# Value products of a fused attention kernel: issued after the second maximum and score of their half step, not between the two

## The chip, the cores and the metric

The kernel runs on one core of one Trainium2 chip. The metric is the device time of one launch in microseconds (us). Engines are named as in the profile: PE is TensorE (PEld its weight loads), DVE is VectorE, ACT is ScalarE, POOL is GpSimd, SP is SyncE.

## The reference

Sixteen sequences of 512 tokens, width 512, pass four residual layers, each on a layer norm of its input: a gated delta rule with 16 heads, a feed-forward layer with routed low-rank adapters, an attention layer, and the feed-forward layer again.

```
x = x + delta_rule(layernorm(x))
x = x + ffn(layernorm(x))
x = x + attn_b(layernorm(x))
x = x + ffn(layernorm(x))

# attn_b, the layer that the change is in (4 groups of queries x 8 key heads, 16 wide)
scores = einsum('bsqhd,bthd->bqhst', qh, kh) * scale
probs  = softmax(scores, axis=-1)
a_dot  = einsum('bqhst,bthd->bsqhd', probs, vh)
a_mem  = sigma_q @ memory / (sigma_q @ memory_norm)
out    = a_dot * (1 - w) + a_mem * w
```

## The kernel before

The program has two parts. The first is the delta rule layer over all 16 sequences; it leaves its result in memory. The second, `token_layers`, does the other three layers, one sequence (a batch) after the other, in a hardware loop of eight passes with two batches each. The change is in the attention of the second part and so runs 16 times.

Attention has 32 query heads. For each head the softmax needs a maximum for every query, and the kernel computes the score matrix twice: once with queries on the partitions, to take the maxima (`maximum`, L1333: one 128x512 matmul for each of four blocks of 128 queries, read by a DVE reduction, L1611), and once with keys on the partitions and the negated maximum already inside the operand (`score`, L1346: one 128x512 matmul for each of four blocks of keys, read by an ACT exponential, L1165, which writes `probs`). `values` (L1358) multiplies the exponentials of four heads with the values, four matmuls side by side, each 32 rows of the output; it does this in four blocks for a quad of heads, one for each block of keys, and adds them up in PSUM bank 6.

All engines run lists written in order. PE's is one Python loop over g = 0 to 44, with two half steps j = 0, 1 for each g. In half step j PE does two maxima of head g and two scores of head g - 7. In this text a **pair** is one maximum with the score issued behind it; a half step has two pairs and a g has four. The pattern repeats every four g, which makes sixteen pairs; they are numbered here 0 to 15 from a g that leaves 3 when divided by 4. In that cycle also stand:

- four value blocks, **V0 to V3**, in the half steps that `AV_SLOTS` names: the second half step of the first three g (pairs 2 and 3, 6 and 7, 10 and 11) and the first one of the fourth (pairs 12 and 13);
- **TURN** (L1405), four transposes of the finished quad, at the end of the first g, behind pair 3, and behind them the DVE's `av_rc` (L1601) and `av_n` (L1605) and POOL's addition (L1067);
- **MAXT** (L1385), four small transposes of the maxima, between the maximum and the score of pair 6. ACT copies them negated into `shift` (L1172), and SP moves that by DMA into the row of `q_stack` that the scores use three g later.

Waits that matter: scores use PSUM banks 0 to 2 in turn, so score m waits for the exponential of score m - 3 (L1345). Maxima use banks 3 to 5, so maximum m waits for the reduction of maximum m - 3 (L1332). MAXT and TURN share bank 7, so MAXT waits for `av_n`. `probs` has room for seven heads (`PROBS = 7`), so the first exponential of heads 7, 11, ..., 31 waits until V3 of a quad has read what it will overwrite:

```
if h >= PROBS and tt == 0:
    act.wait_ge(av_mm, at(b, QUADS, (h - PROBS) // 4 + 1))
```

Those heads are scored in the very g whose first half step holds V3: the exponential that waits is that of pair 12. Behind the exponentials of pairs 12 and 13, and ahead of that of pair 14, ACT's list has the copy of the finished values, `av_sb` (L1178), which V0 and TURN wait for. There are seven such heads in each batch. Five of them come while maxima still run (g = 14, 18, 22, 26, 30), and two later (g = 34, 38), since maxima end with g = 31 and scores with g = 38.

Of the kernel before, what the change touches and what calls it, by code (L numbers as in the profile page):

```python
# [847 lines left out]
QUADS = NQ * NKV // 4  # L848
# [6 lines left out]
AV_LAG = SCORE_LAG + 1  # L855
AV_SLOTS = ((0, 1), (1, 1), (2, 1), (3, 0))
# [9 lines left out]
def token_layers(nc, dims, x2_in, w_ffn, b_ffn, lora_b, gate_b, w_q, w_kv, mem_aug_in, mem_w_in, ident_in, rank_mask_in, sel_in, head_rows_in, out):  # L866
# [3 lines left out]
    with ExitStack() as ctx:  # L870
# [100 lines left out]
        def at(b, per, k):  # L971

            return b * per + k
# [7 lines left out]
        def turned_before(quad):  # L981

            return sum(4 * q + 3 + TURN_LAG < 4 * quad + MAXT_LAG for q in range(QUADS))

        def maxima_before(quad):

            return sum(4 * q + MAXT_LAG <= 4 * quad + 3 + TURN_LAG for q in range(QUADS))
# [197 lines left out]
        def _(pe):  # L1185
# [23 lines left out]
            with pe.Fori(0, NBATCH // 2) as bb:  # L1209
                for par in range(2):  # L1210
# [84 lines left out]
                    def pick_q(m):  # L1295
                        n, hp = divmod(m, HP)
                        if hp == 0:
                            pe.wait_ge(qlo_ready, at(b, NQ, n + 1))
                        bank = stack_bank(HP + m)
                        pe.matmul(ps[:, bank, :], sel[:, hp, :], q_hi[:, n, :], start=True, stop=False)  # L1300
                        pe.matmul(ps[:, bank, :], sel[:, HP + hp, :], q_lo[:, n, :], start=False, stop=True).then_inc(qsel_mm, 1)  # L1301
# [3 lines left out]
                    def memory(t):  # L1305

                        if t == 0:
                            pe.wait_ge(qelu_ready, at(b, NQ, NQ))
                            pe.wait_ge(qlo_ready, at(b, NQ, NQ))
                            pe.wait_ge(shift_ready, at(b, QUADS, 1))  # L1310
                        else:
                            pe.wait_ge(amem_ready, at(b, NT, t))
                        for n in range(NQ):
                            c0 = (DKV + 1) * (n % 2)
                            last = pe.matmul(ps[:, 6 + n // 2, c0:c0 + DKV + 1], q_elu[:, n, P * t:P * t + P],  # L1315
                                             mem_aug[:, :], start=True, stop=True)
                        last.then_inc(mem_mm, 1)

                    def pair(h):

                        n, kv = divmod(h, NKV)
                        return n * HP + kv // 2, kv

                    def maximum(g, st):

                        qt, kv = pair(g)
                        m = NT * g + st
                        if m in (1, 2):
                            pe.wait_ge(qrelu_ready, at(b, NQ, m))
                            pe.wait_ge(qlo_ready, at(b, NQ, m))  # L1330
                        elif m >= MAX_BANKS:
                            pe.wait_ge(max_ready, at(b, NT * NH, m - MAX_BANKS + 1))  # L1332
                        pe.matmul(ps[:, STACK_BANKS + m % MAX_BANKS, :], q_stack[:, qt, P * st:P * st + P], k_stack[:, kv, :],  # L1333
                                  start=True, stop=True).then_inc(max_mm, 1)

                    def score(h, tt):

                        qt, kv = pair(h)
                        if h == 0 and tt == 0:
                            pe.wait_ge(qstack_ready, at(b, NQ * HP, NQ * HP))  # L1340
                        if h % 4 == 0 and tt == 0:
                            pe.wait_ge(shift_in, at(b, 64 * QUADS, 64 * (h // 4 + 1)))
                        m = NT * h + tt
                        if m >= STACK_BANKS:
                            pe.wait_ge(exp_ready, at(b, NT * NH, m - STACK_BANKS + 1))  # L1345
                        pe.matmul(ps[:, m % STACK_BANKS, :], k_stack[:, kv, P * tt:P * tt + P], q_stack[:, qt, :],  # L1346
                                  start=True, stop=True).then_inc(score_mm, 1)

                    def values(quad, tt):

                        if quad == 0 and tt == 0:
                            pe.wait_ge(v_ready, at(b, 1, 1))
                        pe.wait_ge(exp_ready, at(b, NT * NH, NT * (4 * quad + 3) + tt + 1))
                        if tt == 0 and quad:
                            pe.wait_ge(av_ready, at(b, QUADS, quad))
                        for e in range(4):
                            h = 4 * quad + e
                            last = pe.matmul(ps[32 * e:32 * e + 32, 6, :], v_aug[:, tt, h % NKV, :], probs[:, h % PROBS, tt, :],  # L1358
                                             start=tt == 0, stop=tt == NT - 1)
                        if tt == NT - 1:  # L1360
                            last.then_inc(av_mm, 1)

                    for g in range(NH + OUT_LAG):
                        h = g - SCORE_LAG
                        for j in range(2):
                            first = 1 + 2 * g + j
                            if g < SCORE_LAG:
                                pick_q(first)
                                if first == 2 * SCORE_LAG:
                                    pick_q(first + 1)  # L1370
                            if g < NH:
                                if g % 2 == 0 and j == 0:
                                    pe.wait_ge(qstack_ready, at(b, NQ * HP, pair(g)[0] + 1))
                                maximum(g, 2 * j)
                            quad, i = divmod(g - MAXT_LAG, 4)
                            if i == 0 and j == 1 and 0 <= quad < QUADS:
                                pe.wait_ge(max_ready, at(b, NT * NH, 16 * quad + 16))
                                if quad:
                                    pe.wait_ge(shift_ready, at(b, QUADS, quad))
                                if quad == 1:  # L1380
                                    pe.wait_ge(amem_ready, at(b, NT, NT))
                                if turned_before(quad):
                                    pe.wait_ge(avn_ready, at(b, QUADS, turned_before(quad)))
                                for st in range(NT):
                                    last = pe.transpose(ps[0:4, 7, P * st:P * st + P], smax[:, 4 * quad:4 * quad + 4, st], ident2[:, :])  # L1385
                                last.then_inc(maxT_mm, 1)
                            if 0 <= h < NH:
                                score(h, 2 * j)
                            quad, i = divmod(g - 3 - AV_LAG, 4)
                            if (i, j) in AV_SLOTS and 0 <= quad < QUADS:  # L1390
                                values(quad, AV_SLOTS.index((i, j)))
                            if g < NH:
                                maximum(g, 2 * j + 1)
                            if 0 <= h < NH:
                                score(h, 2 * j + 1)
                            if j == 0 and 0 <= g - MEM_LAG < NT:
                                memory(g - MEM_LAG)
                        quad, i = divmod(g - 3 - TURN_LAG, 4)
                        if i == 0 and 0 <= quad < QUADS:
                            pe.wait_ge(av_ready, at(b, QUADS, quad + 1))  # L1400
                            pe.wait_ge(shift_ready, at(b, QUADS, maxima_before(quad)))
                            if quad:
                                pe.wait_ge(avn_ready, at(b, QUADS, quad))
                            for t in range(NT):
                                last = pe.transpose(ps[:, 7, P * t:P * t + P], av_sb[:, P * t:P * t + P], ident2[:, :])  # L1405
                            last.then_inc(avT_mm, 1)
# [297 lines left out]
```

## Time and profile before

| | before |
|---|---|
| runs | 6206.04 us median of 3 (6198.69 to 6215.28) |
| profiled execution | 6172.9 us; its span 6171.1 us |
| mean granted PE clock over the span | 0.863 of full speed |
| PE busy | 5294.1 us (86%) |
| DVE busy | 3719.4 us (60%) |
| ACT busy | 2440.8 us (40%) |
| POOL busy | 909.4 us (15%) |

The delta rule takes the first 17 of the page's 40 slices, the batches of `token_layers` the rest. Busy shares are averages over stages with different limits, so the attention has to be read by itself, in the order of time. A row of the timeline gives the start in us, how long the row's instructions took together, the engine, the line, what is written and read, and how many instructions are merged; in brackets stands how long the engine was idle before, and what ended that. A matmul's own duration includes the time in which its last results leave the array while the next one already streams, so the pace of PE is read from the distance between starts.

### The profile page before, as it was taken

What the parts mean: (1) busy time and instruction counts of PE and PEld (TensorE: products, weight loads), DVE (VectorE), ACT (ScalarE), POOL (GpSimd) and SP (SyncE); (2) the same over time, 40 slices, a digit from 0 to 9 for tenths busy, and PEclk for the clock granted to TensorE, in tenths of its full rate; (3) what the DMA queues carried; (4) which work ended last, traced back from release to release, by engine and by line L of the source; (5) the groups of instructions that cost most, each with busy time, mean ns of one, the idle gap of its engine ahead of it and who ended that gap; (6) DMA issues with size and microseconds to landing.
All of it is one profiled execution on the core that took longest, in us unless ns stands there. A gap on an engine that the chain in (4) does not pass through costs nothing.

```text
span 6171.1 us, 155296 instructions
## 1 busy us (share of the span) xinstructions
PE 5294.1 (86%) x62928; PEld 3907.6 (63%) x62928; DVE 3719.4 (60%) x7900; ACT 2440.8 (40%) x4497; POOL 909.4 (15%) x1075
## 2 busy tenths in 40 slices
PE   4888888888888888498998898898899889889888
PEld 3777777777777777355556556555555555655655
DVE  3555555555555556375666566567567566656656
ACT  2222222222222222153553464454455346346445
POOL 0111111111111111012112112111111210211111
PEclk8777777777777777599999999999999999999999
DMA  2211121211222121100000000000000000000000
GB/s 57 59 47 47 51 54 47 56 45 51 52 54 54 49 53 47 60 1 15 15 1 15 15 1 15 15 2 15 15 15 1 15 15 1 15 15 1 15 15 8
DMA packets 352466, 173.37 MB, mean 28 GB/s; under 512 B 300016, under 2 KB 300784, under 8 KB 350992
## 3 DMA queue, kind: packets, MB, share of 16 engines
q1 hardware_dynamic: 343056, 146.25, 8.9%
q10 hardware_dynamic: 8704, 16.78, 0.8%
q8 instruction: 556, 9.11, 0.6%
q14 instruction: 150, 1.23, 0.1%
HBM read 94.27 MB, written 67.63 MB: 26 GB/s over the span
## 4 chain that ended last, share of the span: by engine, by line
issue 28%; PE 19%; DVE 7%; POOL 3%; ACT 1%; DMA 0%; DVEq 0%; POOLq 0%; SPq 0%; ACTq 0%
PE row_psum L40 5%; PE row_psum L42 5%; PE row_psum L41 5%; DVE smax L1611 2%; POOL xs L1067 2%; PE row_psum L1196 1%; PE row_psum L1333 1%; DVE stats L1437 1%; PE row_psum L1300 1%; POOL rstd L1039 1%; PE row_psum L1301 1%; PE row_psum L1315 1%; DVE xr_lo L1466 0%; DVE xs L1540 0%; DVE probs L1448 0%
## 5 line engine op out<-in xcount | busy, mean ns | idle before, releaser
L1611 DVE TENSOR_REDUCE smax<-row_psum 128x1 f32<-128x512 f32 x2048 | 1281.1, 683 | 314.8 <-PE row_psum L1333 313.9
L1165 ACT ACTIVATE probs<-row_psum 128x512 f32<-128x512 f32 x2048 | 1112.2, 602 | 509.4 <-PE row_psum L1346 404.9
L1333 PE MATMUL row_psum<-k_stack,q_stack 128*128 128x512 f32 x2048 | 878.6, 440 | 28.1 <-DVE smax L1611 24.4
L1346 PE MATMUL row_psum<-q_stack,k_stack 128*128 128x512 f32 x2048 | 841.0, 425 | 23.8 <-ACT probs L1165 13.7
L1333 PEld LDWEIGHTS row_psum<-k_stack,q_stack 128*128 128x128 f32 x2048 | 397.8, 195 | 462.9 <-DVE smax L1611 387.7
L1358 PE MATMUL row_psum<-probs,v_aug 128*32 128x512 f32 x4096 | 538.9, 604 | 9.2 <-ACT av_sb L1178 9.2
L1346 PEld LDWEIGHTS row_psum<-q_stack,k_stack 128*128 128x128 f32 x2048 | 383.2, 192 | 255.1 <-ACT probs L1165 195.6
L733 DVE TENSOR_TENSOR lane_t<-lane_t,lane_p 128x30 f32<-128x30 f32 (+14 forms) x960 | 408.8, 426 | 33.0
L748 DVE TENSOR_TENSOR tri<-span_bank,masks 128x512 f32<-128x512 f32 x256 | 156.0, 681 | 381.5 <-PE span_bank L505 381.5
L358 ACT ACTIVATE uw<-span_bank 128x512 f32<-128x512 f32 x256 | 152.9, 597 | 564.4 <-PE span_bank L525 454.3
L730 DVE TENSOR_TENSOR lane_p<-lane_t 128x30 f32<-128x30 f32 (+14 forms) x960 | 340.0, 354 | 30.8
L525 PE MATMUL span_bank<-rhs,inv_b 32*32 32x64 f32 x4096 | 220.5, 301 | 154.1 <-issue 88.4
L40 PE MATMUL row_psum<-wf_hi,xr_hi 128*128 128x320 f32 (+1 forms) x1024 | 327.5, 320 | 14.2 <-DVE xr_lo L1466 13.3
L1196 PE MATMUL row_psum<-ident,probs 128*128 128x128 f32 x784 | 170.9, 375 | 180.2 <-DVE probs L1448 180.2
L42 PE MATMUL row_psum<-wf_hi,xr_lo 128*128 128x320 f32 (+1 forms) x1024 | 323.9, 316 | 0.0
L41 PE MATMUL row_psum<-wf_lo,xr_hi 128*128 128x320 f32 (+1 forms) x1024 | 323.6, 316 | 0.0
L1067 POOL TENSOR_TENSOR xs<-xs,av_n 128x256 f32<-128x256 f32 x128 | 93.2, 728 | 1557.2 <-DVE av_n L1605 1557.2
L525 PEld LDWEIGHTS span_bank<-rhs,inv_b 32*32 32x32 f32 x4096 | 210.3, 165 | 164.5 <-issue 164.5
L40 PE MATMUL span_bank<-x_hi,w_hi 128*128 128x256 f32 x1024 | 301.1, 294 | 3.0 <-DVE x_lo L712 3.0
L41 PE MATMUL span_bank<-x_lo,w_hi 128*128 128x256 f32 x1024 | 287.4, 281 | 0.0
L42 PE MATMUL span_bank<-x_hi,w_lo 128*128 128x256 f32 x1024 | 287.0, 280 | 0.0
L1085 ACT ACTIVATE xr_hi<-row_psum 128x512 fp32r<-128x512 f32 x196 | 112.0, 600 | 400.8 <-PE row_psum L1196 400.8
(204 smaller groups left out, 10804.8 us busy)
## 6 DMA issues: line engine op xcount, KB each, us to landing
xs<-x SPq DMA_DIRECT2D x17, 1024.0 KB, 5.5
x_sp<-in_x ACTq DMA_DIRECT2D x32, 512.0 KB, 3.4
tri_dram<-tri SPq DMA_DIRECT2D x256, 64.0 KB, 2.1
lane_t<-tri_dram SPq DMA_DIRECT2D x32, 512.0 KB, 4.1
inv_dram<-lane_t SPq DMA_DIRECT2D x32, 512.0 KB, 2.6
inv_b<-inv_dram SPq DMA_DIRECT2D x256, 64.0 KB, 2.3
x_res<-in_x SPq DMA_DIRECT2D x32, 512.0 KB, 4.7
x<-x_res SPq DMA_DIRECT2D x32, 512.0 KB, 2.8
```

Source lines behind the costliest of these rows:

```text
L40: pe.matmul(out, a_hi, b_hi, start=first, stop=False)
L41: pe.matmul(out, a_hi, b_lo, start=False, stop=False)
L42: return pe.matmul(out, a_lo, b_hi, start=False, stop=last)
L525: return pe.matmul(bank[4 + q][r, 2 * HD * (h % 8):2 * HD * (h % 8) + 2 * HD], inv_b[r, t, h, :], rhs[r, s, t, h, :], start=True, stop=True)
L730: mark(dve.tensor_tensor(prod, lane_t[:, 0:m, m:m + 1].to_broadcast([P, m, n]), lane_t[:, m:m + 1, m + 1:NB].to_broadcast([P, m, n]), ALU. ...
L733: mark(dve.tensor_tensor(lane_t[:, 0:m, m + 1:NB], lane_t[:, 0:m, m + 1:NB], prod, ALU.add))
L1165: act.activation(probs[:, h % PROBS, tt, :], ps[:, m % STACK_BANKS, :], ACT.Exp, scale=float(DH) ** -0.5).then_inc(exp_ready, 1)
L1196: last = pe.transpose(ps[:, t, P * k:P * k + P], xn[:, t, P * k:P * k + P], ident2[:, :])
L1333: pe.matmul(ps[:, STACK_BANKS + m % MAX_BANKS, :], q_stack[:, qt, P * st:P * st + P], k_stack[:, kv, :], start=True, stop=True).then_inc(m ...
L1346: pe.matmul(ps[:, m % STACK_BANKS, :], k_stack[:, kv, P * tt:P * tt + P], q_stack[:, qt, :], start=True, stop=True).then_inc(score_mm, 1)
L1358: last = pe.matmul(ps[32 * e:32 * e + 32, 6, :], v_aug[:, tt, h % NKV, :], probs[:, h % PROBS, tt, :], start=tt == 0, stop=tt == NT - 1)
L1611: dve.tensor_reduce(smax[:, g, st:st + 1], ps[:, STACK_BANKS + (NT * g + st) % MAX_BANKS, :], AX.X, ALU.max).then_inc(max_ready, 1)
```

## The change

Two calls trade places inside the half step. Everything that a half step issues is the same, and only PE's list differs.

```
                             if 0 <= h < NH:
                                 score(h, 2 * j)
-                            quad, i = divmod(g - 3 - AV_LAG, 4)
-                            if (i, j) in AV_SLOTS and 0 <= quad < QUADS:
-                                values(quad, AV_SLOTS.index((i, j)))
                             if g < NH:
                                 maximum(g, 2 * j + 1)
                             if 0 <= h < NH:
                                 score(h, 2 * j + 1)
+                            quad, i = divmod(g - 3 - AV_LAG, 4)
+                            if (i, j) in AV_SLOTS and 0 <= quad < QUADS:
+                                values(quad, AV_SLOTS.index((i, j)))
                             if j == 0 and 0 <= g - MEM_LAG < NT:
                                 memory(g - MEM_LAG)
```

The first place is PE's list at V3, in g = 14 (L1332 prepares the number that the maximum waits for, L1333 is a maximum, L1346 a score, L1358 a value block). Before, from pair 12 on:

```order
L1332 REGISTER_ALU [waits qstack_ready]
L1333 MATMUL row_psum<-k_stack,q_stack 128x512 [waits max_ready]
L1346 MATMUL row_psum<-q_stack,k_stack 128x512 [waits exp_ready]
L1358 MATMUL row_psum<-probs,v_aug 32x512 [waits exp_ready]
L1358 MATMUL row_psum<-probs,v_aug 32x512 x3
L1332 REGISTER_ALU
L1333 MATMUL row_psum<-k_stack,q_stack 128x512 [waits max_ready]
L1346 MATMUL row_psum<-q_stack,k_stack 128x512 [waits exp_ready]
```

Now, from pair 12 on:

```order
L1332 REGISTER_ALU [waits qstack_ready]
L1333 MATMUL row_psum<-k_stack,q_stack 128x512 [waits max_ready]
L1346 MATMUL row_psum<-q_stack,k_stack 128x512 [waits exp_ready]
L1332 REGISTER_ALU
L1333 MATMUL row_psum<-k_stack,q_stack 128x512 [waits max_ready]
L1346 MATMUL row_psum<-q_stack,k_stack 128x512 [waits exp_ready]
L1358 MATMUL row_psum<-probs,v_aug 32x512 [waits exp_ready]
L1358 MATMUL row_psum<-probs,v_aug 32x512 x3
```

Pair 13 stands ahead of V3 now, and six pairs instead of seven lie between V3 and the next V0.

The second place is PE's list at V0 and TURN, in g = 15 (L1405 is TURN). Before, from the score of pair 2 on:

```order
L1346 MATMUL row_psum<-q_stack,k_stack 128x512 [waits exp_ready]
L1358 MATMUL row_psum<-probs,v_aug 32x512 [waits av_ready,exp_ready]
L1358 MATMUL row_psum<-probs,v_aug 32x512 x3
L1332 REGISTER_ALU
L1333 MATMUL row_psum<-k_stack,q_stack 128x512 [waits max_ready]
L1346 MATMUL row_psum<-q_stack,k_stack 128x512 [waits exp_ready]
L1405 MATMUL row_psum<-ident,av_sb 128x128 [waits avn_ready,shift_ready,av_ready]
L1405 MATMUL row_psum<-ident,av_sb 128x128 x3
```

Now, from the score of pair 2 on:

```order
L1346 MATMUL row_psum<-q_stack,k_stack 128x512 [waits exp_ready]
L1332 REGISTER_ALU
L1333 MATMUL row_psum<-k_stack,q_stack 128x512 [waits max_ready]
L1346 MATMUL row_psum<-q_stack,k_stack 128x512 [waits exp_ready]
L1358 MATMUL row_psum<-probs,v_aug 32x512 [waits av_ready,exp_ready]
L1358 MATMUL row_psum<-probs,v_aug 32x512 x3
L1405 MATMUL row_psum<-ident,av_sb 128x128 [waits avn_ready,shift_ready,av_ready]
L1405 MATMUL row_psum<-ident,av_sb 128x128 x3
```

Pair 3 stands ahead of V0 now, and TURN directly behind it. V1 and V2 move behind pairs 7 and 11 in the same way. The lists of DVE, ACT, POOL and SP are the same in both kernels.

## Rows read from the trace of the kernel before

**Rows 1.** The page, part 1: busy time, share of the span, instructions of each engine

```profile
PE 5294.1 (86%) x62928; PEld 3907.6 (63%) x62928; DVE 3719.4 (60%) x7900; ACT 2440.8 (40%) x4497; POOL 909.4 (15%) x1075
```

**Rows 2.** Windows of one attention: busy us by engine, then PE clock and DMA

```profile
4024.80:4104.00 79.20, 75.14 (x386) 42.66 (x388) 64.00 (x117) 51.75 (x98) 7.24 (x7) 0.98 0.01 2
```

**Rows 3.** Waits, 2650 to 6171 us: who waited for whom, us in total, times, longest

```profile
ACT probs L1165 <- PE row_psum L1346: 404.9, 565, 4.9
...
DVE smax L1611 <- PE row_psum L1333: 313.9, 468, 2.0
...
PEld row_psum L1346 <- ACT probs L1165: 195.6, 388, 0.8
...
ACT probs L1165 <- PE row_psum L1358: 99.4, 112, 1.0
```

**Rows 4.** Timeline, PE, one cycle from V3 to the next V3

```profile
4085.95 1.06 PE L1358 MATMUL row_psum<-probs,v_aug 128*32 128x512 f32 x8
4086.95 0.50 PE L1333 MATMUL row_psum<-k_stack,q_stack 128*128 128x512 f32 x1
...
4088.00 0.40 PE L1333 MATMUL row_psum<-k_stack,q_stack 128*128 128x512 f32 x1
...
4088.93 0.40 PE L1333 MATMUL row_psum<-k_stack,q_stack 128*128 128x512 f32 x1
4089.36 0.50 PE L1346 MATMUL row_psum<-q_stack,k_stack 128*128 128x512 f32 x1
4089.70 0.39 PE L1333 MATMUL row_psum<-k_stack,q_stack 128*128 128x512 f32 x1
4089.93 0.42 PE L1346 MATMUL row_psum<-q_stack,k_stack 128*128 128x512 f32 x1
4090.28 1.06 PE L1358 MATMUL row_psum<-probs,v_aug 128*32 128x512 f32 x8
...
4091.84 0.60 PE L1405 MATMUL row_psum<-ident,av_sb 128*128 128x128 f32 x4
4092.19 0.48 PE L1333 MATMUL row_psum<-k_stack,q_stack 128*128 128x512 f32 x1
...
4099.37 1.06 PE L1358 MATMUL row_psum<-probs,v_aug 128*32 128x512 f32 x8
```

**Rows 5.** Timeline, ACT, behind the same V3

```profile
4087.15 1.18 ACT L1165 ACTIVATE probs<-row_psum 128x512 f32<-128x512 f32 x2 [0.95 <-PE row_psum L1358]
4088.22 0.59 ACT L1178 ACTIVATE av_sb<-row_psum 128x512 f32<-128x512 f32 x1
4088.70 2.56 ACT L1165 ACTIVATE probs<-row_psum 128x512 f32<-128x512 f32 x5
```

**Rows 6.** Timeline, DVE, behind the same V3

```profile
4087.49 3.68 DVE L1611 TENSOR_REDUCE smax<-row_psum 128x1 f32<-128x512 f32 x6 [0.84 <-PE row_psum L1333]
```

**Rows 7.** Timeline, PE, the end of the attention, without maxima

```profile
4113.79 0.50 PE L1333 MATMUL row_psum<-k_stack,q_stack 128*128 128x512 f32 x1
...
4118.68 0.60 PE L1405 MATMUL row_psum<-ident,av_sb 128*128 128x128 f32 x4
...
4120.18 0.60 PE L1385 MATMUL row_psum<-ident,smax 128*4 128x128 f32 x4 [0.45 <-DVE av_n L1605]
...
4126.21 1.89 PE L1346 MATMUL row_psum<-q_stack,k_stack 128*128 128x512 f32 x4
...
4137.34 1.34 PE L1346 MATMUL row_psum<-q_stack,k_stack 128*128 128x512 f32 x3
...
4140.25 0.65 PE L1405 MATMUL row_psum<-ident,av_sb 128*128 128x128 f32 x4
4140.84 2.78 PE L1358 MATMUL row_psum<-probs,v_aug 128*32 128x512 f32 x24
```

**Rows 8.** Timeline, ACT, behind V3 of g = 34

```profile
4126.41 1.09 ACT L1165 ACTIVATE probs<-row_psum 128x512 f32<-128x512 f32 x2 [0.72 <-PE row_psum L1358]
4127.38 0.60 ACT L1178 ACTIVATE av_sb<-row_psum 128x512 f32<-128x512 f32 x1
```

More of the change, by code:

```diff
@@ L1388, in _ @@
                                 score(h, 2 * j)
-                            quad, i = divmod(g - 3 - AV_LAG, 4)
-                            if (i, j) in AV_SLOTS and 0 <= quad < QUADS:
-                                values(quad, AV_SLOTS.index((i, j)))
                             if g < NH:
@@ L1395, in _ @@
                                 score(h, 2 * j + 1)
+                            quad, i = divmod(g - 3 - AV_LAG, 4)
+                            if (i, j) in AV_SLOTS and 0 <= quad < QUADS:
+                                values(quad, AV_SLOTS.index((i, j)))
                             if j == 0 and 0 <= g - MEM_LAG < NT:
```

## The prediction

> **What bounds the kernel now.** I read the page's busy shares first: PE 86%, DVE 60%, ACT 40% [rows 1]. A share over four layers does not say what limits the attention, so next the window over most of one attention: PE busy 75.1 of 79.2 us, DVE 64.0, ACT 51.8, the clock at 0.98 of full speed, which is its upper level, 2.4 GHz [rows 2]. PE sets the pace there. The waits agree: ACT was idle 404.9 us for scores and DVE 313.9 us for maxima [rows 3], so both usually have time to spare, and relieving either is worth something only where PE then waits for it.
>
> Third, PE in the order of time, one cycle of sixteen pairs [rows 4]. From one V3 to the next it takes 13.42 us (4085.95 to 4099.37). In a plain stretch two pairs cost 0.93 (4088.00 to 4088.93), one pair 0.47, one matmul about 0.235. Two kinds of distance are longer. Beside a value block: V0 starts 0.35 after the score ahead of it, a block takes 1.00 (4085.95 to 4086.95), and the two pairs behind it 1.05 (4086.95 to 4088.00), so the first of them 0.58. And one wait: the maximum of pair 1 starts at 4088.93 and its score at 4089.36, 0.43 instead of 0.23. After this wait the next distance is 0.34. I find nothing else in the cycle at which PE waits.
>
> What is the wait for? ACT's rows behind V3 [rows 5]. The exponential of pair 12 may not start until V3 is done; it starts at 4087.15, 0.20 behind V3's end. Pair 13 follows, then the copy `av_sb` at 4088.22, then pair 14 at 4088.70. The score of pair 1 needs the bank of pair 14, and starts 0.66 after that exponential's start. So a chain hangs on V3: V3's end, two exponentials, the copy, a third exponential, score 1, in all 2.41 us (4086.95 to 4089.36). PE has work for all but 0.20 of it. ACT waited for V3 112 times, 99.4 us [rows 3]: seven times in each of 16 batches, 0.89 us each. **This chain joins the two engines once in each cycle**, and a cycle is its length plus the time that PE needs from score 1 to the end of the next V3.
>
> **The change, part by part.** It adds and removes no instruction; it moves four value blocks behind one more pair each. No queue of SP or POOL is touched.
>
> *V3.* The chain starts at the end of V3, and V3 now has pair 13 ahead of it. On PE, from score 1 to V3's end, there were eleven pairs, V0 to V3, TURN and MAXT; now there are twelve. PE does not wait in that stretch, so it grows by one pair: **+0.47**. What the pair leaves behind is one pair less beneath the chain, where PE was waiting anyway: the wait before score 1 becomes longer, and nothing is won. That is the core of the forecast: the pair moves from a stretch with slack to one without.
>
> *The chain itself.* Score 13 now precedes V3, so its exponential need not wait for it. Before, the two exponentials and the start of the copy span 1.07 us (4087.15 to 4088.22); where both scores already lay ready, behind V3 of g = 34, 0.97 (4126.41 to 4127.38) [rows 8]. The chain gets shorter by up to 0.10, to 2.31 or 2.33: **-0.08**. Can a stall lie beneath it that lasts longer? Score 15 needs exponential 12 (free at 0.20 + 0.66 = 0.86 behind V3; PE comes at 0.80), score 0 exponential 13 (1.35, PE 1.33), both far ahead of 2.33. The maxima: six reductions take 3.68 us, 0.61 each, from 0.54 behind V3 [rows 6]; maximum 3 needs the reduction of maximum 0, done at about 2.4, and comes at 3.14.
>
> *V0 and TURN.* Behind score 1 stand pairs 2 and 3 and V0. Before: 2.48 us from score 1 to TURN (4089.36 to 4091.84). Now 0.34, four plain matmuls less one (3 x 0.235 - 0.01, about 0.69), 0.34 into V0, 1.00: 2.37, so -0.11. Score 3 needs exponential 0, free at 3.29 behind V3, and comes at 3.37: close, so up to +0.10 for a restart. TURN then directly follows V0, with its first load not hidden. Before it costs 0.35 to the next matmul (4091.84 to 4092.19). The only TURN behind a value block is at 4140.25, 0.59 before the value block that follows [rows 7], in which the step into a value block is contained. Bounds 0.35 and 0.59; I take 0.46, nearer to the first since 0.1 belongs to that step: +0.11. Together **0.00**. MAXT waits for `av_n`, and comes no earlier than 1.50 behind TURN (4118.68 to 4120.18, where it was held [rows 7]). In the cycle two and a half pairs lie between: 0.35 + 5 x 0.235, at least 1.53, and now 0.1 more. That cover stays.
>
> *V1, V2.* Their steps in and out are as many as before, and score and maximum beside them only change places. **0**, with ±0.05.
>
> A cycle thus grows by 0.47 - 0.08 + 0.00 = 0.39 us, to 13.8.
>
> *One batch.* V3 of g = 14 comes one pair later: +0.47. Four cycles follow (g = 18 to 30): 4 x 0.39 = 1.56. From V3 of g = 30 to that of g = 34 (4113.79 to 4126.21, 12.42 us [rows 7]) the maxima have run out, and MAXT, held by `av_n`, and ACT's copy of it are last; the pair more counts as a score alone, 0.2 to 0.3 with its waits, the gains at the chain and before TURN return 0.2: -0.02 net. From g = 34 to 38 (11.13 us, 4126.21 to 4137.34) only scores are left, and PE follows the exponentials at their pace of 0.49 (2.56 less 0.60 for the last, over four [rows 5]). V3 behind one more score comes one exponential later: **+0.49**. What follows that V3 is unchanged.
>
> Sum: 0.47 + 1.56 - 0.02 + 0.49 = 2.50 us in a batch, **times 16 = +40 us**. Against the profiled execution's own 6172.9 that gives 6213. The median of the runs is 6206.0, 33 us above the profiled execution; the difference carries over as it is: **6246 us** (+0.64%).
>
> PE's price for a pair deserves a doubt. Rows 4 show 0.235 us between plain starts. The Trainium skill, page "TensorE: Matmul & The Clock Gate", section "Back-to-back issue gap", gives about 131 ns for a sustained stream at 512 columns; by that the pair would cost 0.26 instead of 0.47, and the sum would be about 20 us. The trace does not agree with that figure, and the rows decide.
>
> Unknown costs, both ends. The moved pair: nothing (if the wait swallows it) to 0.58 (what it costs behind a value block). The chain: -0.10 to 0. TURN behind V0: -0.11 to +0.13 on its term. Score 3's restart: 0 to 0.10. Without the first, whose lower end is the second rival, they make 22 to 58 us.
>
> **Rivals.**
>
> *Faster: ready banks feed ACT and DVE through each value block.* Before, one fresh score and one fresh maximum stand ahead of a block of 1 us; now two. ACT and DVE idle less behind each block (404.9 and 313.9 us in all [rows 3]). If ACT's lead reached around to the chain, PE's wait at score 1 would go: 0.20 and its restart 0.11, five times, 1.55 us a batch, 25 us: 6181. It decides if exponential 12 no longer waits for V3. For it: PE's loads waited for ACT 195.6 us in all. Against it: ACT waits a full 0.95 for V3 [rows 5], and V3 now comes later in the list. Chance 0.09.
>
> *No change.* If something ahead of V3 had slack, V3 would end at the same time as before, with its pair in a gap. Speaks for it: PE's total work is the same. Against it: there is no distance above plain ones between 4089.70 and 4099.37 that a value block or a transpose does not explain. 6206. Chance 0.14.
>
> *Twice the restarts.* If scores 15, 0 and 3 each miss their exponential slightly, PE restarts up to three times a cycle, and TURN costs its upper 0.59: +0.10 + 0.13 a cycle, five times, 16 batches, 18 us more: 6264. Chance 0.13.
>
> My forecast has 0.64. Faster by over 0.3% gets 0.09, within 0.3% 0.14, slower 0.77; 0.3% (19 us) is about what a measurement of this kernel tells from no change. The likeliest case alone reaches from 6228 to 6264. For eight in ten I stretch down towards no change, and up for the scatter of the runs: 6208 to 6268.
>
> **What would show it.** Right: POOL's addition of `av_n` comes every 13.8 us in the middle of a batch, not 13.4. ACT's wait for V3 grows from 0.95 to about 1.4, in all from 99.4 to about 150 us. Score 1 starts 2.3 behind V3's end, 0.7 behind maximum 1 instead of 0.43. In the end part the distance of the two V3 grows from 11.13 to 11.6. PE's busy time stays. Wrong: if score 1 comes without a longer wait, the chain is not what binds; if a cycle is 14 or more, restarts or DVE have joined; if a cycle is 13.4, there was slack ahead of V3.

## The result and the profile after

The changed kernel is slower: 6257.25 us median of 4 runs (6250.64 to 6262.6) against 6202.44 of the kernel before, a ratio of 1.0084 with a 95% interval of 1.0064 to 1.0104. On another chip, with more runs, it was 1.0088 (1.0073 to 1.0103). Forecast were +40 us (+0.64%); it is +55 us, inside the range.

The profiled executions differ by 90 us (6262.6 against 6172.9), and 32 us of that lie ahead of the attention: the first addition of `av_n` starts at 2733.6 us before and at 2765.3 after, though the change moves only the first V0 to V3 there, for which half a microsecond a batch was worked out. The part ahead of the attention moves from profile to profile of the same code (a second profile of the changed kernel has 2746.6), so from here on stretches are compared within the attention. From the first addition of `av_n` to the last (16 batches) it is 3400.9 us before and 3459.5 after: +58.6, or 3.66 a batch.

PE's busy time and the waits of the changed kernel, in the same columns as [rows 1, 3]:

```profile
PE 5347.4 (85%) x62928; PEld 3900.4 (62%) x62928; DVE 3721.0 (59%) x7900; ACT 2413.2 (39%) x4497; POOL 909.3 (15%) x1075
```
```profile
ACT probs L1165 <- PE row_psum L1346: 333.7, 385, 4.9
...
ACT probs L1165 <- PE row_psum L1358: 262.5, 112, 2.6
DVE smax L1611 <- PE row_psum L1333: 252.8, 371, 2.1
PEld row_psum L1346 <- ACT probs L1165: 231.5, 514, 0.8
```

ACT and DVE do wait less for scores and maxima (404.9 to 333.7 and 313.9 to 252.8): two ready banks ahead of each value block feed them as the first rival said. ACT waits 163 us more for V3, and PE's loads more often for ACT (388 to 514 times).

One middle cycle on PE, to be held beside [rows 4]:

```profile
2785.63 1.06 PE L1358 MATMUL row_psum<-probs,v_aug 128*32 128x512 f32 x8
2786.63 0.50 PE L1333 MATMUL row_psum<-k_stack,q_stack 128*128 128x512 f32 x1
...
2787.19 0.40 PE L1333 MATMUL row_psum<-k_stack,q_stack 128*128 128x512 f32 x1
2787.48 0.50 PE L1346 MATMUL row_psum<-q_stack,k_stack 128*128 128x512 f32 x1
2787.81 0.40 PE L1333 MATMUL row_psum<-k_stack,q_stack 128*128 128x512 f32 x1
2788.06 0.47 PE L1346 MATMUL row_psum<-q_stack,k_stack 128*128 128x512 f32 x1
2788.37 0.39 PE L1333 MATMUL row_psum<-k_stack,q_stack 128*128 128x512 f32 x1
2788.94 0.50 PE L1346 MATMUL row_psum<-q_stack,k_stack 128*128 128x512 f32 x1 [0.19 <-ACT probs L1165]
...
2789.51 0.42 PE L1346 MATMUL row_psum<-q_stack,k_stack 128*128 128x512 f32 x1
2789.77 0.40 PE L1333 MATMUL row_psum<-k_stack,q_stack 128*128 128x512 f32 x1
2790.01 0.41 PE L1346 MATMUL row_psum<-q_stack,k_stack 128*128 128x512 f32 x1
2790.35 1.07 PE L1358 MATMUL row_psum<-probs,v_aug 128*32 128x512 f32 x8
2791.35 0.66 PE L1405 MATMUL row_psum<-ident,av_sb 128*128 128x128 f32 x4
2791.76 0.48 PE L1333 MATMUL row_psum<-k_stack,q_stack 128*128 128x512 f32 x1
...
2799.38 1.06 PE L1358 MATMUL row_psum<-probs,v_aug 128*32 128x512 f32 x8
```

V3 to V3 is 13.75 us (13.42 before). V3's end to score 1 is 2.31 (2786.63 to 2788.94; 2.41 before), though one pair less lies beneath: the score now stands 0.57 behind its maximum, not 0.43. (Between V3 and the next V0 there are six pairs in both kernels, 13 to 2 before and 14 to 3 now, not seven before as the text on the change says; the pair less is between V3 and score 1.) TURN, directly behind V0, costs 0.41 to the next matmul (0.35 before). ACT behind the same V3, beside [rows 5]:

```profile
2786.83 1.08 ACT L1165 ACTIVATE probs<-row_psum 128x512 f32<-128x512 f32 x2 [2.54 <-PE row_psum L1358]
2787.80 0.61 ACT L1178 ACTIVATE av_sb<-row_psum 128x512 f32<-128x512 f32 x1
2788.27 2.09 ACT L1165 ACTIVATE probs<-row_psum 128x512 f32<-128x512 f32 x4
```

The start of the first exponential is 0.20 behind V3 as before, and the copy starts 0.97 later, not 1.07.

The end part brought what was not forecast. PE in the first batch, V3 of g = 34, V0 and TURN of g = 35, and the same three in the third batch:

```profile
2825.65 1.07 PE L1358 MATMUL row_psum<-probs,v_aug 128*32 128x512 f32 x8
...
2830.38 1.94 PE L1358 MATMUL row_psum<-probs,v_aug 128*32 128x512 f32 x8
2832.24 1.12 PE L1405 MATMUL row_psum<-ident,av_sb 128*128 128x128 f32 x4
...
3277.62 1.06 PE L1358 MATMUL row_psum<-probs,v_aug 128*32 128x512 f32 x8
...
3282.34 1.07 PE L1358 MATMUL row_psum<-probs,v_aug 128*32 128x512 f32 x8
3283.34 0.66 PE L1405 MATMUL row_psum<-ident,av_sb 128*128 128x128 f32 x4
```

The value block takes 1.94 us in one and 1.07 in the other. Windows from V0 of g = 31 to V0 of g = 35 and from there past TURN, for both batches (columns as in [rows 2]):

```profile
2817.84:2830.38 12.54, 11.05 (x58) 3.99 (x57) 1.33 (x4) 9.21 (x20) 0.72 (x1) 1.00 0.01 1
2830.38:2833.01 2.63, 2.63 (x13) 0.97 (x13) 0.00 (x0) 0.98 (x2) 0.00 (x0) 0.50 0.02 6
3269.81:3282.34 12.53, 11.04 (x57) 3.99 (x56) 1.33 (x4) 9.21 (x20) 0.73 (x1) 1.00 0.01 1
3282.34:3284.92 2.58, 2.36 (x17) 1.04 (x16) 0.68 (x2) 1.64 (x5) 0.09 (x1) 1.00 0.03 6
```

In the first batch the granted clock falls to 0.50, the lower level of 1.2 GHz, as V0 starts, at the end of the stretch in which PE waited for exponentials (in the other batches that fall it is 0.4 to 0.7 us earlier, among the last scores of that stretch); in the third it stays at 2.4 GHz, although PE was busy for the same 11.0 us before. This happens in 8 of 16 batches and costs 1.5 us each. In the kernel before it never happens in this stretch.

### The profile page after: what moved, and what is told of

Same layout as the page of the kernel before. It is cut to its first block, busy times and chain, and to the rows that moved or that the text cites. A ratio compares the mean times of both kernels' runs of the same rounds, so it can differ in the third digit from the quotient of the medians.

```text
span 6260.8 us, 155296 instructions
## 1 busy us (share of the span) xinstructions
PE 5347.4 (85%) x62928; PEld 3900.4 (62%) x62928; DVE 3721.0 (59%) x7900; ACT 2413.2 (39%) x4497; POOL 909.3 (15%) x1075
## 4 chain that ended last, share of the span: by engine, by line
issue 28%; PE 19%; DVE 7%; POOL 3%; ACT 1%; DMA 0%; DVEq 0%; POOLq 0%; SPq 0%; ACTq 0%
PE row_psum L40 5%; PE row_psum L42 4%; PE row_psum L41 4%; DVE smax L1611 2%; POOL xs L1067 1%; PE row_psum L1196 1%; PE row_psum L1333 1%; DVE stats L1437 1%; POOL rstd L1039 1%; PE row_psum L1300 1%; PE row_psum L1315 1%; PE row_psum L1301 1%; DVE xr_lo L1466 0%; DVE xs L1540 0%; DVE probs L1448 0%
## 5 line engine op out<-in xcount | busy, mean ns | idle before, releaser
L1611 DVE TENSOR_REDUCE smax<-row_psum 128x1 f32<-128x512 f32 x2048 | 1279.5, 682 | 259.2 <-PE row_psum L1333 252.8
L1165 ACT ACTIVATE probs<-row_psum 128x512 f32<-128x512 f32 x2048 | 1079.6, 614 | 598.6 <-PE row_psum L1346 333.7
L1346 PE MATMUL row_psum<-q_stack,k_stack 128*128 128x512 f32 x2048 | 863.3, 434 | 48.7 <-ACT probs L1165 42.4
L1333 PE MATMUL row_psum<-k_stack,q_stack 128*128 128x512 f32 x2048 | 868.2, 434 | 28.1 <-DVE smax L1611 24.4
L1333 PEld LDWEIGHTS row_psum<-k_stack,q_stack 128*128 128x128 f32 x2048 | 395.5, 194 | 381.9 <-DVE smax L1611 317.7
L1346 PEld LDWEIGHTS row_psum<-q_stack,k_stack 128*128 128x128 f32 x2048 | 386.4, 193 | 331.7 <-ACT probs L1165 231.5
L1358 PE MATMUL row_psum<-probs,v_aug 128*32 128x512 f32 x4096 | 546.0, 611 | 9.1 <-ACT av_sb L1178 9.1
L1601 DVE RECIPROCAL av_rc<-row_psum 128x16 f32<-128x16 f32 x128 | 32.9, 257 | 490.2 <-PE row_psum L1405 490.2
```

Of the source, the lines that this page charges most:

```text
L1165: act.activation(probs[:, h % PROBS, tt, :], ps[:, m % STACK_BANKS, :], ACT.Exp, scale=float(DH) ** -0.5).then_inc(exp_ready, 1)
L1611: dve.tensor_reduce(smax[:, g, st:st + 1], ps[:, STACK_BANKS + (NT * g + st) % MAX_BANKS, :], AX.X, ALU.max).then_inc(max_ready, 1)
```

## The experiments

The code cuts are shortened: the calls are those of the kernel, and conditions that do not change are left out.

The starts of POOL's addition of `av_n` behind the TURNs are a ruler through every batch. Means over the 16 batches of each profile, in us; "falls" counts the batches in which the distance from g = 31 to 35 is over 1 us longer than in the others:

| kernel | middle cycle | g = 31 to 35 | g = 35 to 39 | falls | first to last | ratio to before (95%) |
|---|---|---|---|---|---|---|
| before | 13.42 | 12.10 | 9.52 | 0 | 3400.9 | |
| the change | 13.76 | 13.29 | 10.21 | 8 | 3459.5 | 1.0084 (1.0064, 1.0104) |
| the change, again | 13.77 | 13.41 | 10.19 | 9 | 3466.2 | 1.0088 (1.0073, 1.0103) |
| V3 only | 13.79 | 12.81 | 9.76 | 5 | 3450.8 | 1.0077 (1.0058, 1.0096) |
| V0 to V2 only | 13.38 | 12.31 | 9.96 | 0 | 3412.1 | 1.0008 (0.9993, 1.0023) |
| V3 ahead of pair 12 | 13.44 | 12.19 | 9.62 | 0 | 3402.7 | 1.0011 (0.9998, 1.0023) |
| V3 behind pair 14 | 14.25 | 13.20 | 10.51 | 2 | 3498.4 | 1.0156 (1.0140, 1.0173) |
| change for g < 32 | 13.77 | 12.10 | 9.51 | 0 | 3438.0 | 1.0055 (1.0035, 1.0075) |
| change for g >= 32 | 13.41 | 12.97 | 10.20 | 5 | 3433.3 | 1.0046 (1.0033, 1.0058) |
| change, PE kept busy | 13.77 | 12.53 | 10.18 | 0 | 3448.2 | 1.0084 (1.0056, 1.0111) |
| the same, again | 13.77 | 12.54 | 10.18 | 0 | 3454.4 | 1.0082 (1.0060, 1.0105) |
| before, copy later | 13.24 | 11.76 | 9.52 | 0 | 3384.4 | 0.9973 (0.9959, 0.9988) |
| change, copy later | 13.77 | 13.41 | 10.19 | 9 | 3462.8 | 1.0095 (1.0065, 1.0124) |

"First to last" holds some us of scatter from the layers between, so the distances decide and the ratios confirm.

**Which of the four blocks.** Theory A is the prediction's chain on V3, theory B a small cost at each block. V3 alone behind:

```
 score(h, 2 * j)
-if (i, j) in AV_SLOTS: values(...)
+if (i, j) in AV_SLOTS[:-1]: values(...)      # V0 to V2
 maximum(g, 2 * j + 1); score(h, 2 * j + 1)
+if (i, j) == AV_SLOTS[-1]: values(...)       # V3
```

> V3 alone stands behind pair 13; V0, V1 and V2 stay between their pairs as in the kernel before. Theory A (the chain that hangs on V3's end): nearly the whole loss is here. A middle cycle grows by 0.37 us (+0.47 for the pair, -0.10 for the chain) to 13.8 us, the wait of ACT for V3 goes from 0.95 to 2.5 us in the cycle, and the time is +0.6 to +0.9% over before (+38 to +55 us, the upper end if PE's clock falls in the end part as it does in the changed kernel). Theory B (each value block costs a little, by whichever queue is starved behind it): a quarter of the loss, about +13 us (+0.2%), a middle cycle of 13.5.

Measured: 13.79 us a cycle, ratio 1.0077. ACT's wait for V3 in the cycle is 1.42 us; I had expected 2.5. Then the other three:

```
-if (i, j) in AV_SLOTS: values(...)
+if (i, j) == AV_SLOTS[-1]: values(...)       # V3
 maximum(g, 2 * j + 1); score(h, 2 * j + 1)
+if (i, j) in AV_SLOTS[:-1]: values(...)      # V0 to V2
```

> V0, V1 and V2 stand behind both maxima and scores, V3 stays between its pairs. Theory A: no loss; the middle cycle stays at 13.4 us (within 0.05), the time within 0.2% of before. Theory B: three quarters of the loss, +40 us (+0.65%), a middle cycle of 13.7.

Measured: 13.38, and 1.0008 with an interval that holds 1. V3 carries the whole loss of the middle cycles, and theory B falls there. It does not fall in the end part: V0 to V2 alone lengthen g = 31 to 39 by 0.21 + 0.44 us, V3 alone (in the batches without a fall) by 0.23 + 0.24; together they are the changed kernel's 0.44 + 0.68. ACT's wait of 2.54 in the changed kernel can be read from this too: 1.42 comes with V3, and the other 1.1 with V0 to V2, since V2 behind pair 11 lets exponential 11 be done a block earlier. It moves nothing.

**One pair earlier, and two pairs later.** V3 ahead of the maximum of pair 12:

```
+if (i, j) == AV_SLOTS[-1]: values(...)       # V3
 maximum(g, 2 * j); ...; score(h, 2 * j)
-if (i, j) in AV_SLOTS: values(...)
+if (i, j) in AV_SLOTS[:-1]: values(...)      # V0 to V2
```

> V3 stands one pair earlier than before, ahead of pair 12; the rest as before. If the loss were simply V3's place in PE's list, one pair earlier would win what one pair later loses: a middle cycle of 13.0 us and -0.6% (-40 us). Theory A says no: the first exponential behind V3 then waits for its own score, which V3 now precedes (0.34 + 0.44 = 0.78 behind V3's end), so the chain grows by the 0.49 that the pair saves; the cycle stays at 13.4 us, and only the two V3 without maxima beside them give something back: 0 to -15 us (0 to -0.25%).

Measured: 13.44, ratio 1.0011. PE and ACT behind V3:

```profile
2776.93 1.06 PE L1358 MATMUL row_psum<-probs,v_aug 128*32 128x512 f32 x8
2777.93 0.50 PE L1333 MATMUL row_psum<-k_stack,q_stack 128*128 128x512 f32 x1
...
2780.81 0.50 PE L1346 MATMUL row_psum<-q_stack,k_stack 128*128 128x512 f32 x1
```
```profile
2778.69 1.09 ACT L1165 ACTIVATE probs<-row_psum 128x512 f32<-128x512 f32 x2 [1.05 <-PE row_psum L1346]
```

ACT now waits for the score, and starts 0.76 behind V3's end; score 1 comes 2.88 behind it, not 2.41. The pair saved is given back by the chain. The gain of up to 15 us that I expected of the end part did not come: its two distances grew by 0.1 each. V3 behind pair 14:

```
-if (i, j) in AV_SLOTS: values(...)
+if (i, j) in AV_SLOTS[:-1]: values(...)      # V0 to V2, between the pairs as before
+if (i, j) == (3, 1): values(...)             # V3, between pairs 14 and 15
```

> V3 one pair later than with V3 alone moved: behind pair 14, V0 to V2 as before. A dose of two pairs. Theory A: the chain from V3's end to the score of pair 1 stays 2.31 us, the stretch from there to the next V3 grows by another pair, so a middle cycle is 13.79 + 0.47 = 14.26 us, and the time some +1.3 to +1.6% over before. If the loss came from V3 being directly ahead of a new half step, or from a bank left empty once, the second pair would cost less than half of the first: 13.8 to 14.0.

Measured: 14.25, ratio 1.0156.

```profile
2764.77 1.06 PE L1358 MATMUL row_psum<-probs,v_aug 128*32 128x512 f32 x8
2765.77 0.49 PE L1333 MATMUL row_psum<-k_stack,q_stack 128*128 128x512 f32 x1
2766.61 0.50 PE L1346 MATMUL row_psum<-q_stack,k_stack 128*128 128x512 f32 x1 [0.35 <-ACT probs L1165]
...
2768.08 0.50 PE L1346 MATMUL row_psum<-q_stack,k_stack 128*128 128x512 f32 x1 [0.18 <-ACT probs L1165]
```

Score 1 stands 2.31 behind V3's end once more, as the third pair behind V3; in the kernel before it is the fifth. Each pair ahead of V3 costs a pair.

**The middle and the end.** The change for g < 32 only, and from 32 on only:

```
+if g < 32 (or g >= 32): V behind both pairs
+else:                   V between, as before
```

> The change for g below 32 only; from g = 32 on, where maxima have run out, the order of the kernel before. Expected from the middle of each batch: +0.35 at its start and four cycles of +0.35, 1.8 us a batch, 28 us (+0.45%), and from TURN of g = 31 to TURN of g = 35 and of g = 39 the distances of before, 12.1 and 9.5 us. No fall of PE's clock in the end part. If the end part were not a cause of its own, the time would be that of the changed kernel, +0.84%.

> The change from g = 32 on only. Expected: middle cycles of 13.42 us; the distances of the last additions of av_n grow from 12.1 to 12.5 and from 9.5 to 10.2 us, 1.1 us a batch or 18 us, and another 1.5 us in those batches in which PE's clock falls behind V3 of g = 34 (8 of 16 in the changed kernel, 12 us): +18 to +30 us (+0.3 to +0.5%).

Measured: 13.77 with 12.10 and 9.51 behind it; and 13.41 with 12.97 and 10.20, five falls. By these distances the two parts are independent, and about half of the loss is the end part's. The ratios (1.0055 and 1.0046) add up to more than the whole change's 1.0084, within their intervals.

**The clock.** The changed kernel with five unread matmuls a batch:

```
+def keep_busy():
+    pe.matmul(ps[:, STACK_BANKS + 1, :], q_stack[:, 0, 0:P], k_stack[:, 0, :], start=True, stop=True)
 score(h, 2 * j)
+if (g, j) in ((34, 1), (35, 0), (35, 1)): keep_busy()
 maximum(g, 2 * j + 1); score(h, 2 * j + 1)
+if (g, j) in ((34, 1), (35, 0)): keep_busy()
```

> The changed kernel with five matmuls of 128x512 more in each batch, whose results nobody reads, each behind a score of g = 34 or 35 in the stretch in which PE waits for ACT. If PE's clock falls because PE idles there, it stays at 1.00 in all 16 batches, V0 of g = 35 takes 1.06 us and not 1.94, the distance TURN to TURN is 12.5 us in all batches, and the time is 12 us under that of the changed kernel (+0.65% over before instead of +0.84%). If the fall has another cause, about half of the batches still show 14.0 us, and the time is that of the changed kernel or more by up to 5 x 0.23 x 16 = 18 us.

> The changed kernel with the five unread matmuls a batch, once more, beside the changed kernel. If the fall of the clock is what it costs in the end part, it is faster than change_again by 12 us (0.2%) and takes 3448 us from the first addition of av_n to the last, with 12.5 us between the TURNs of g = 31 and 35 in all batches.

> The changed kernel itself, once more, on the same chip as the two beside it: +0.6 to +1.0% over before; V0 of g = 35 at the lower clock in about half of the batches, 3460 us from the first addition of av_n to the last.

In both profiles all 32 batches take 12.5 us, where the changed kernel has 17 falls in 32. From the end of V3 of g = 34 to V0 of g = 35, in the first batch of the changed kernel and of this one, and here on past TURN:

```profile
2826.65:2830.38 3.73, 2.89 (x11) 1.12 (x7) 0.00 (x0) 3.54 (x8) 0.00 (x0) 1.00 0.00 0
2795.82:2799.55 3.73, 3.43 (x16) 1.68 (x12) 0.00 (x0) 3.53 (x8) 0.00 (x0) 1.00 0.00 0
2799.55:2802.12 2.57, 2.35 (x16) 1.03 (x16) 0.68 (x2) 1.63 (x5) 0.09 (x1) 1.00 0.03 6
```

PE is busy for 3.43 us of the same 3.73 instead of 2.89: more work in the gaps, and no delay. First to last is 11 to 12 us shorter than with the change alone. The time I had expected (+0.65%) did not show in the ratios: 1.0082 and 1.0088 on one chip overlap and do not settle it, though the medians there were 6227.3 and 6244.2 us. So idle PE time is a cause of the fall, shown in the traces by taking it away.

What sets a batch that falls apart from one that does not, with the same busy time? In the two profiles of the changed kernel 15 of the 17 falls are in the second batch of a loop pass, the other two in the first batch of all. And they go with another fall of the clock, near the start of each attention: in the clock records it begins 84.0 to 84.5 us ahead of V3 of g = 34 in all 17 batches that fall, and over 85 us ahead in 14 of the 15 that do not; the last has none there. With the five matmuls it begins 84.0 to 84.5 us ahead in 14 of 32 batches, and none of them falls, so the matmuls did not merely shift this. Why the place of the earlier fall matters stays open.

**The copy on ACT.** In both kernels, for the first six quads:

```
-if (i, j) == AV_SLOTS[-1] and 0 <= quad < QUADS:
+if (i, j) == ((3, 1) if quad < 6 else AV_SLOTS[-1]) and 0 <= quad < QUADS:
     ...
     act.activation(av_sb[:, :], ps[:, 6, :], ACT.Copy)
```

> The kernel before with one edit on ACT: the copy av_sb stands behind the exponentials of pairs 14 and 15, not ahead of them, for the first six quads. Theory A: the chain loses the copy (0.48 us), so PE no longer waits at the score of pair 1 (0.20 and its restart 0.11): the middle cycle shrinks from 13.42 to 13.1 us, the time by about 0.3 x 5 x 16 = 24 us (-0.4%). A theory in which PE alone sets the cycle, with its pauses beside value blocks, expects no change (13.42).

> The changed kernel with the copy av_sb behind the exponentials of pairs 14 and 15, as tried on the kernel before. Theory A: the chain behind V3 is four exponentials and the copy long for the score of pair 3, whichever way they stand; score 1 comes 0.4 us sooner, score 3 then waits, from 3.38 to 3.29 us behind V3's end. The middle cycle shrinks by only 0.1 us, to 13.7, the time by about 7 us against the changed kernel, where the same edit wins 0.3 us a cycle on the kernel before. If the edit won the same on both, it would be 13.45 and 24 us.

On the kernel before: 13.24 and a ratio of 0.9973 (0.9959 to 0.9988), the one version that beats both. The cycle lost 0.18, not 0.31, and PE's rows tell why:

```profile
2760.79 0.41 PE L1333 MATMUL row_psum<-k_stack,q_stack 128*128 128x512 f32 x1
2761.03 0.40 PE L1346 MATMUL row_psum<-q_stack,k_stack 128*128 128x512 f32 x1
2761.29 0.19 PEld L1333 LDWEIGHTS row_psum<-k_stack,q_stack 128*128 128x128 f32 x1 [0.30 <-DVE smax L1611]
2761.29 0.50 PE L1333 MATMUL row_psum<-k_stack,q_stack 128*128 128x512 f32 x1
2761.63 0.40 PE L1346 MATMUL row_psum<-q_stack,k_stack 128*128 128x512 f32 x1
```

Score 1 (2761.03) follows its maximum at the plain 0.24; but maximum 2, whose weight load waited for a DVE reduction, comes 0.03 late, and the next start after a wait is 0.34 away, not 0.23. DVE is the next bound, at once. On the changed kernel the same edit won nothing (13.77, where I had expected 13.7): score 3 came 3.29 behind V3's end, as worked out, but as a wait, so that V0 came 0.43 behind it, not 0.34, and stood where it was, 3.72 behind V3's end.

## Why the prediction was right, and where its sizes were off

The direction and its main mechanism, the pair ahead of V3, are borne out by experiments of their own. That the number fits is in part the width of the range: the first V3 and the middle cycles, worked out at 32 us, came to about 30, but the end part, worked out at 8, came to 28.

*V3, +0.47 for the pair.* Right, and the core of it: shown by V3 alone (13.79), by the dose of two pairs (14.25, worked out 14.26), and by the order with V3 first, which wins nothing.

*The chain, -0.08.* 2.31 against 2.41: -0.10. V3 alone gives the same.

*V0 and TURN, 0.00.* Score 1 to TURN 2.41 (2.37 worked out), TURN to the next matmul 0.41 (0.46): together 2.82 against 2.83. Right, by two small errors of opposite sign.

*V1 and V2, 0.* Right in the cycles (13.38 with V0 to V2 moved). A middle cycle thus grew by 0.34, not 0.39.

*From g = 30 to 34, -0.02.* 12.53 against 12.43: +0.10.

*From g = 34 to 38, +0.49.* This term was mis-sized. V3 to V3 is 12.00 us in the third batch (3277.62 to 3289.62), +0.88. I had priced V3 alone and put V0 to V2 at nothing, and it is the other way round. In the third batch of each run V3 alone makes it 11.34, +0.22: the score that moves ahead of V3 starts 0.24 behind the one before it, without a wait, and V3 to V0 stays 4.24 us with that score gone from it. V0 to V2 alone make it 11.77, +0.65. There the score that moves ahead of V0 comes at the pace of the exponentials, +0.49, which is the step that I had given to V3. And four scores now follow TURN ahead of V1, where three did. The fourth has to wait for its exponential; before, V1 ran beneath that time. Before, and with the change:

```profile
4130.79 0.60 PE L1405 MATMUL row_psum<-ident,av_sb 128*128 128x128 f32 x4
4131.14 0.99 PE L1346 MATMUL row_psum<-q_stack,k_stack 128*128 128x512 f32 x3
4132.07 1.06 PE L1358 MATMUL row_psum<-probs,v_aug 128*32 128x512 f32 x8
```
```profile
3283.34 0.66 PE L1405 MATMUL row_psum<-ident,av_sb 128*128 128x128 f32 x4
3283.75 0.94 PE L1346 MATMUL row_psum<-q_stack,k_stack 128*128 128x512 f32 x3
3284.92 0.50 PE L1346 MATMUL row_psum<-q_stack,k_stack 128*128 128x512 f32 x1 [0.22 <-ACT probs L1165]
3285.35 1.06 PE L1358 MATMUL row_psum<-probs,v_aug 128*32 128x512 f32 x8
```

From TURN to V1 it is 2.01 us instead of 1.28, +0.73; between V0 and TURN one score less gives back 0.34. The stretch from V1 to V2 has the same wait in both kernels and does not change.

*The clock.* Not in the forecast at all: 8 falls of 1.5 us, 12 us in the profile. I had read 0.98 for the attention before and taken it as fixed, while adding idle time to PE in the stretch where it was already idle most.

*The sum.* Worked out 2.50 us a batch; found 4 x 0.34 + 0.10 + 0.88 + 0.77 (the clock, mean) = 3.1, against the 3.66 of the ruler. The 0.5 left over is about the 0.47 worked out for the first V3, but it is no measurement of it: from the attention's first matmul to that V3 the mean is 20.46 us against 19.65, and that stretch scatters by over 1 us between the batches of one profile. The forecast +40, the ratio says +52 (40 to 64).

*The rivals.* "Ready banks" names something real: ACT and DVE do wait less. It is worth nothing, since neither sets the pace. "No change" falls with V3 alone. "Twice the restarts" has a price, 58 us, near what was measured, by luck. Scores 15 and 0 do restart in the cycle (0.33 behind 2787.48, 0.31 behind 2788.06), but beneath the chain, where it costs nothing, score 3 (2790.01) does not wait, and TURN costs 0.41; the rest of the loss is in the end part.

*What would show it.* A cycle of 13.8 and score 1 at 2.3 came true. ACT's wait for V3 was to be 1.4 and was 2.54; 1.42 is what V3 alone gives, and I had not seen that V2 behind pair 11 adds to it. In all it was to be 150 us: V3 alone gives 143.9, the change 262.5. PE's busy time was to stay and grew by 53 us (5294.1 to 5347.4). Of that 22 lie ahead of the first V0; in a middle cycle it grows from 13.39 to 13.56, since a score behind a wait is recorded with 0.50 us and not 0.40.

## What to carry to other kernels

Look for the place where the engine that sets the pace starts a chain on another engine and later waits for its end. Work moved ahead of the chain's start costs its full price; work moved out from beneath the chain returns nothing. An engine's idle total (ACT waited 163 us more here, for a loss of 55) says little of what an order costs; one cycle laid out in time, with each start after a wait priced, says nearly all. Then lay out the stretches that are unlike it, first and last, with the same care: here they held half of the loss and nearly all of the error.

## What the runs showed of the hardware

- A 128x512 matmul of this kernel's scores starts 0.235 us behind the one before it; the first one behind a wait or a value block is followed only 0.34 us later. That 0.11 us comes on top of the wait, and a short wait can cost it in full: in the kernel before with the copy later, 0.03 us of lateness cost 0.14. There the weight load was released together with its matmul (both 2761.29). Where the load is released earlier it costs less: that of the score at 2789.51 had waited for ACT until 2789.43, and the next start is 0.26 away.
- PE's clock fell to 1.2 GHz at the end of a stretch of 12.5 us in which PE was busy for 11.05, in 17 of 32 batches; the longest idle time listed there is 0.43 us. With five more matmuls in the waits it fell in none of 32. The Trainium skill, page "TensorE: Matmul & The Clock Gate", section "A second HAM failure mode: psum-queue depth-cycling", describes this for a bf16 kernel at 512 columns: short idle times between groups of matmuls that cycle through PSUM banks make the clock swing between its two levels. The trace agrees in kind; here it is one fall in about half of the batches.
